# Weight splitting at seven jobs per five slots, a later input chain for the second pair, and the low-part branch at slot 24

## The chip, the cores and the metric

One core of one Trainium2 chip runs the whole program. The metric is device microseconds of one execution, and the time of a kernel is the median of its runs. A profiled execution has its own time and a span, from the first to the last of the program's instructions.

## The reference, cut to what matters

A transformer block on x of 16 sequences x 256 tokens x 256 features: attention with 16 heads of 128, then a mixture of 64 experts, each behind a layernorm and each followed by one. The change touches the attention alone:

```python
w = codes * jnp.repeat(scales, block_size, axis=0)      # wq, wk, wv: 256 x 2048; wo: 2048 x 256
q = x @ w_q + bq;  k = x @ w_k + bk;  v = x @ w_v + bv   # x is layernorm(input)
scores = jnp.einsum('bqhd,bkhd->bhqk', q, k) / jnp.sqrt(128)
attn = jax.nn.softmax(scores, axis=-1)
out = jnp.einsum('bhqk,bkhd->bqhd', attn, v)
return out @ w_o + bo
```

## The kernel before, in words

**Tiling.** The 16 sequences go as 8 pairs (bp), each with 16 heads, so there are 128 items i = bp * 16 + head, and two units u (one per sequence of the pair) for each item: 256 units. The attention is a software pipeline of slots, one unit per slot. Every engine walks the same slots in order and does, in each, what the tables ORDER (lines 45 to 57) list for even and odd slots, each with its lag. An even slot of TensorE holds nearly everything for two units: scores of u and u+1 (L1029), the Q and K projection of a later head (L1000), the output projection (L1061), a V projection (L1015), and the product of probabilities and V (L1044). I call an even slot with the odd one behind it a pair of slots. VectorE takes row maxima (L1397), reciprocals (L1393), copies K out (L1372) and makes the low halves of V (L1377) and O (L1403). ScalarE does the exponentials (L1259), the high half of P (L1268), Q (L1230), V (L1237) and O (L1251). GpSimd normalises P (L931, "norm") and makes its low half (L936, "P"): in an odd slot norm(u-1), norm(u), P(u-1), P(u). SyncE issues the transposing DMA of P (L798, "T"), one unit per slot, with a lag of one slot, behind the slot's "bg" work.

**Passes.** Operands are split into a high and a low fp16 part, and a product takes three passes (high*high, high*low, low*high). The weights come as codes times scales and mostly fit the high part alone. A flag says whether any low part is nonzero; if none is, PE leaves out the pass over the weight's low part (`passes`, L981). Slots 0 to 31 always take three passes. In front of slot 32 PE waits for the flag (L1082), reads it and branches.

**Weight jobs.** 32 jobs (`w_job`, L478) make the split weights. Each is two loads of 128 x 512 f32 (codes and scales, 256 KB each, L489 or L492) into a ring of NST = 8 stages, a multiply on GpSimd (L506), a high part on ScalarE (L510), a low part on VectorE (L514), and on VectorE an OR of the low part's bits into `lowbits` (L521). Jobs below 6 run ahead of the slots; 6 to 13 stand at slots 0, 1, 1, 2, 3, 3, 4, 4, and job n from 14 on at slot n - 10, so the last is at slot 21. The loads are issued in the same slot as the multiply, in SyncE's "bg" part, which in an odd or even slot stands before T of the unit before. ScalarE's part is one slot later and VectorE's two slots later for n of 14 and above. The load of job n waits until job n - 8 has made its low part.

**Flag.** `flag_jobs` (L531) reduces `lowbits` on VectorE at slot 25, transposes it on PE at slot 27 (L537), and reduces again at slot 28 (L538, L540).

**Input chain.** `x_jobs(bp)` (L450) computes the layernorm of pair bp and transposes it into XT: small VectorE steps (L357 to L388), four ScalarE steps (L392), and twice a PE transpose (L423) with its high and low copies (L427, L429). It is spread by the table PLACE["x"] over slots base + 1 to base + 14 with base = (bp - 1) * 32. For bp = 1 its products are first used by V in slot 26 and by Q and K in slot 30. A K projection waits for the last use of its bank bP1 in front of it, so it waits for a transpose's low copy.

**Zero fills.** SyncE also fills BUF in DRAM with zeros in slots 24, 26, 28 and 30 (L808, 1926 KB each), behind the slot's T, and Y from slot 32 on (L823, 512 KB each). They go through the same SyncE DMA queue as T.

Of the kernel before, what the change touches and what calls it, by code (L numbers as in the profile page):

```python
# [18 lines left out]
E = 64  # L19
CAP = 96  # L20
NST = 8
SCALE = 128.0 ** -0.5

SX, SW, SV, SP_, SO = 4.0, 4.0, 2.0, 64.0, 128.0
# [69 lines left out]


TURN_X = (11, 13)
PE_AT = (17, 19, 23, 31)
STORE_AT = (18, 20)
KEEP_AT = (22, 24)
# [26 lines left out]
def places(chain, base):  # L126

    left = {who: iter(slots) for who, slots in PLACE[chain].items()}

    def at(who):  # L130
        slot, j = next(left[who])
        return base + slot, j

    return at
# [49 lines left out]
def build(nc, x, wc, wsc, wo_c, wo_s, bqkv, bo, gateT, sguT, sdT, ewT, ewd, out):  # L184
    ctx = ExitStack()
    with ctx:
# [249 lines left out]
        def k_read(slot):  # L436

            return (s["kl"], sum(i < FIRST["K"] or k_place(i) < pe_place(slot, "bg") for i in range(NI)))
# [11 lines left out]
        def x_jobs(bp):  # L450
            g = bp % 4
            base = (bp - 1) * 32

            def load(eng):
                if bp >= 4:
                    eng.wait_ge(s_x1[bp % 2], 32 * ((bp - 4) // 2 + 1))
                eng.dma_start(X[:, g, :, :], x[bp * 512:(bp + 1) * 512, :].rearrange("(t p) d -> p t d", p=128)
                              ).then_inc(s_x[g], 16)

            plan["sp"].setdefault(PRO if bp < 3 else base, []).append(load)  # L460
            at = places("x", base) if bp else first
            put(stats, XC, 0, at, lambda t: X[:, g, t, :], [(s_x[g], 16 * (bp // 4 + 1))])
            put(normal, XC, 0, at, lambda t: XN[:, t, :], lambda t: X[:, g, t, :])
            for c in range(2):
                slot = base + TURN_X[c] if bp else PRO
                w = [k_read(slot)] if bp else [(s["cg"], 2)]
                turn(XC, slot, at, lambda t, c: XN[:, t, c * 128:(c + 1) * 128], c,
                     lambda l, c=c: XT[:, bp % 2, l, c, :], w, [(s["k"], max(0, 16 * (bp - 1)))])
            xt_ready[bp] = XC.n
# [8 lines left out]
        def w_job(n):  # L478
            m, chn, c = wjobs[n]
            b = n % NST  # L480
            slot = PRO if n < 6 else {6: 0, 7: 1, 8: 1, 9: 2, 10: 3, 11: 3, 12: 4, 13: 4}.get(n, n - 10)

            def load(eng):
                if n >= NST:
# [9 lines left out]
                                      ).then_inc(s_st[b], 16)  # L494

            cnt = 2 * (n // NST + 1)
            plan["sp"].setdefault(slot, []).append(load)
            if m < 3:
                o = c * 2048 + chn * 512
            else:  # L500
# [20 lines left out]
                    eng.scalar_tensor_tensor(out=lowbits, in0=lo.bitcast(U32), scalar=NOSIGN, in1=lowbits,  # L521
                                             op0=ALU.bitwise_and, op1=ALU.bitwise_or).then_inc(s["lf"], 1)

            now = n < 14
            plan["pool"].setdefault(PRO if n < NST else slot, []).append(scaled)
            plan["act"].setdefault(slot if now else slot + 1, []).append(high)
            plan["dve"].setdefault(slot if now else slot + 2, []).append(low)
            w_ready[wjobs[n]] = n + 1


        def flag_jobs():  # L531
            def rows(eng):
                eng.wait_ge(s["lf"], 32)
                return eng.tensor_reduce(low1, lowbits, AX, ALU.max)

            LC.step("dve", 25, rows)
            LC.step("pe", 27, lambda e: e.transpose(bP1[0:1, 0:128], low1, ident[:, :]), [k_read(27)])  # L537
            n = LC.step("dve", 28, lambda e: e.tensor_reduce(low2, bP1[0:1, 0:128], AX, ALU.max))  # L538
            p1_busy[27] = (LC.sem, n)
            return LC.step("dve", 28, lambda e: e.tensor_scalar(low3, low2, 1.0, None, ALU.min))  # L540


        ht_ready, acc_free, a_free = {}, {}, {}
# [433 lines left out]
        def _(eng):  # L977
# [100 lines left out]
                for u in slots:  # L1078
                    slot_work("pe", u, work)

            attention(range(0, 32), True)
            eng.wait_ge(s["lc"], LOW_READY)  # L1082
            low = eng.value_load(low3[0:1, 0:1], min_val=0, max_val=1)
            with eng.If(low == 0):
                attention(range(32, END), False)
            with eng.Else():
                attention(range(32, END), True)

            def shared_up(k):
                g, j = divmod(k, 3)  # L1090
# [448 lines left out]
```

## Time and profile before

| | us |
|---|---|
| median of 3 runs | 1377.25 (1375.5 to 1378.28) |
| profiled execution, its own time | 1383.52 |
| its span | 1381.8 |
| PE busy in the span | 1223.8 (89%) |
| POOL busy | 922.2 (67%) |
| DVE busy | 869.4 (63%) |
| ACT busy | 826.4 (60%) |

Start times of slots are read from the first score matmul (L1029) of each even slot on PE's timeline: slot 0 at 37.40, 2 at 44.12, 4 at 54.59, 6 at 70.22, 8 at 78.53, 10 at 87.96, 18 at 128.93, 20 at 137.23, 24 at 156.40, 26 at 164.63, 32 at 189.82, 34 at 196.40 and 36 at 202.90 us. In what follows "s24" is the start of slot 24. Views show engines as PE (matmul), PEld (weight load), DVE (VectorE), ACT (ScalarE), POOL (GpSimd), and SPq (SyncE's queue); "bank" is a PSUM bank, and HT is the memory in which the weight stages lie.

### The profile page before, as it was taken

To read this page: it belongs to the slowest core of one execution; us is meant where nothing else is said; L and a number is where in the kernel's file an instruction comes from. 1 tells how busy PE (TensorE), PEld (TensorE's weight loads), DVE (VectorE), ACT (ScalarE), POOL (GpSimd) and SP (SyncE) were. 2 spreads that over 40 slices of the span, in tenths; PEclk is the share of its full clock that TensorE was granted. 3 is DMA by queue.
4 is the path that set the end of the run, shared out by engine and by line. 5 is a ranking of instruction groups with operands and counts; after the bars stand their busy time and mean duration, and the time that the engine had idled before them with its cause. 6 is when DMAs were issued, how large, how long until landed. Compare 5 with 4: busy or idle time off the path is not lost.

```text
span 1381.8 us, 25355 instructions
## 1 busy us (share of the span) xinstructions
PE 1223.8 (89%) x7876; PEld 855.4 (62%) x7876; DVE 869.4 (63%) x2285; ACT 826.4 (60%) x2128; POOL 922.2 (67%) x1126
## 2 busy tenths in 40 slices
PE   3789999999899999989999998998966998989984
PEld 1455666666566666666666666666634577768863
DVE  5766667677668758777976875777765333223337
ACT  2566668778677767777777677777733332223413
POOL 3576656568877877887887798688755523444554
PEclk9999999999999999999999999999977999999977
DMA  5556796755655444444535444444434569887683
GB/s 189 138 150 171 188 243 165 162 95 120 120 104 107 89 98 96 77 89 93 97 69 91 94 82 79 78 79 80 88 84 132 160 176 239 225 229 206 135 251 122
DMA packets 364678, 182.68 MB, mean 132 GB/s; under 512 B 287440, under 2 KB 343222, under 8 KB 364544
## 3 DMA queue, kind: packets, MB, share of 16 engines
q1 hardware_dynamic: 344960, 166.18, 50.8%
q0 software_dynamic: 16416, 11.70, 4.6%
q10 hardware_dynamic: 3168, 3.15, 0.7%
q8 instruction: 67, 1.10, 0.3%
q14 instruction: 67, 0.55, 0.1%
HBM read 75.32 MB, written 64.69 MB: 101 GB/s over the span
## 4 chain that ended last, share of the span: by engine, by line
PE 40%; DVE 20%; DMA 13%; POOL 12%; issue 7%; ACT 5%; SPq 2%; another core or an unknown queue 0%; ACTq 0%; POOLq 0%; DVEq 0%
PE bank L1029 7%; PE bank L1000 6%; PE bank L1044 6%; DMA PT<-PH 5%; DMA Y<-W,wix 5%; POOL P L931 4%; POOL PH L936 4%; PE bank L1015 4%; DVE nm L1397 3%; PE bank L1061 3%; PE bank L1163 3%; PE bank L1106 3%; PE bank L1176 2%; PE bank L1122 2%; POOL BUF L691 2%
## 5 line engine op out<-in xcount | busy, mean ns | idle before, releaser
L931 POOL TENSOR_SCALAR P<-P,rr 128x256 f32<-128x256 f32 x512 | 245.1, 491 | 148.1 <-DVE rr L1393 139.7
L1259 ACT ACTIVATE P<-bank,nm 128x256 f32<-128x256 f32 x512 | 237.6, 469 | 153.6 <-DVE nm L1397 143.3
L936 POOL TENSOR_TENSOR PH<-P,PH 128x512 f16<-128x512 f32 x256 | 297.7, 1178 | 16.3 <-ACT PH L1268 15.5
L1000 PE MATMUL bank<-RB,W 128*128 128x512 f16 x1092 | 261.0, 382 | 12.4 <-ACT Sx L620 4.1
L691 POOL DMA_INDIRECT BUF<-RT,ix x192 | 198.3, 1033 | 96.3 <-issue 40.9
L1029 PE MATMUL bank<-RB 128*128 128x256 f32 x1024 | 246.4, 384 | 2.9 <-ACT RB L1230 1.7
L1044 PE MATMUL bank<-PT,RB 128*128 128x256 f16 x1536 | 197.7, 274 | 29.8 <-DMA PT<-PH 26.5
L1397 DVE TENSOR_REDUCE nm<-bank 128x2 f32<-128x512 f32 x256 | 174.3, 681 | 53.8 <-PE bank L1029 53.3
L1029 PEld LDWEIGHTS bank<-RB 128*128 128x128 f32 x1024 | 186.4, 192 | 26.5 <-issue 2.7
L1044 PEld LDWEIGHTS bank<-PT,RB 128*128 128x128 f16 x1536 | 146.4, 98 | 88.0 <-DMA PT<-PH 41.5
L1268 ACT ACTIVATE PH<-P 128x512 f16<-128x512 f32 x256 | 161.3, 630 | 59.1 <-POOL P L931 45.7
L1000 PEld LDWEIGHTS bank<-RB,W 128*128 128x128 f16 x1092 | 106.4, 98 | 134.3 <-issue 18.0
L952 POOL DMA_INDIRECT Y<-W,wix x64 | 90.5, 1415 | 124.3 <-ACT W L1330 76.2
L1061 PE MATMUL bank<-W,O 128*128 128x256 f16 x1080 | 142.6, 276 | 30.3 <-DVE O L1403 26.8
L1061 PEld LDWEIGHTS bank<-W,O 128*128 128x128 f16 x1080 | 104.0, 99 | 79.2 <-DVE O L1403 25.9
L1377 DVE SCALAR_TENSOR_TENSOR RB<-bank,RB 128x512 f16<-128x512 f32 x128 | 87.9, 687 | 93.1 <-ACT RB L1237 85.7
L1015 PE MATMUL bank<-W,RB 128*128 128x512 f16 x550 | 140.5, 381 | 3.3 <-DVE RB L1377 3.3
L1259 ACT ACTIVATION_READ_ACCUMULATOR P<-bank,nm 128x1 f32 x512 | 101.1, 197 | 0.0
L1403 DVE SCALAR_TENSOR_TENSOR O<-bank,bqk,O 128x512 f16<-128x512 f32 x128 | 94.8, 740 | 3.6 <-issue 3.2
L1372 DVE TENSOR_SCALAR RB<-bank,bqk 128x512 f32<-128x512 f32 x128 | 95.4, 745 | 1.9 <-PE bank L1000 1.9
L1251 ACT ACTIVATE O<-bank,bqk 128x512 f16<-128x512 f32 x128 | 87.4, 683 | 14.6 <-PE bank L1044 8.4
L1230 ACT ACTIVATE RB<-bank,bqk 128x512 f32<-128x512 f32 x128 | 87.9, 687 | 3.0 <-PE bank L1000 3.0
(200 smaller groups left out, 1609.6 us busy)
## 6 DMA issues: line engine op xcount, KB each, us to landing
RB<-in_ewT SPq DMA_DIRECT2D x24, 352.0 KB
BUF<-zrow SPq DMA_DIRECT2D x4, 1926.0 KB, 8.6
W<-BUF SPq DMA_DIRECT2D x64, 120.4 KB
HT<-in_ewT SPq DMA_DIRECT2D x18, 352.0 KB
HT<-in_wc SPq DMA_DIRECT2D x24, 256.0 KB, 4.2
HT<-in_ws SPq DMA_DIRECT2D x24, 256.0 KB, 4.6
Y<-zrow SPq DMA_DIRECT2D x10, 512.0 KB, 3.2
RB<-in_ewd SPq DMA_DIRECT2D x24, 176.0 KB
```

The source lines that it names most:

```text
L691: eng.indirect_dma_start(BUF, bass.IndirectOffsetOnAxis(ap=ix[:, rt, t, k:k + 1], axis=0), RT[:, rt, t, :], None, bounds_check=CAP * E - 1 ...
L931: r = eng.tensor_scalar(p, p, rr[:, w % 4, t:t + 1], SP_, ALU.mult, ALU.mult)
L936: eng.tensor_tensor(PH[:, w % 2, 1, :], P[:, w % 2, :], PH[:, w % 2, 0, :], ALU.subtract).then_inc(s["pl"], 1)
L1000: r = eng.matmul(bk_[:, :], W[:, m, a, c * 2048 + h * 128:c * 2048 + (h + 1) * 128], XT[:, bp % 2, b, c, :], start=(k == 0), stop=(k == n ...
L1015: r = eng.matmul(bV[:, :], XT[:, bp % 2, a, c, t * 128:(t + 1) * 128], W[:, 2, b, c * 2048 + hg * 512:c * 2048 + (hg + 1) * 512], start=(k ...
L1029: r = eng.matmul(bS[u % 2][:, t * 256:(t + 1) * 256], QK[:, i % 2, 0, q * 256 + t * 128:q * 256 + (t + 1) * 128], QK[:, i % 2, 1, q * 256: ...
L1044: r = eng.matmul(bO[:, q * 256:(q + 1) * 256], V[:, i // 4 % 2, a, 2 * q + kc, h % 4 * 128:(h % 4 + 1) * 128], PT[:, u % 2, b, :, kc, :], ...
L1061: r = eng.matmul(bACC[q][:, t * 256:(t + 1) * 256], O[:, a, q * 256 + t * 128:q * 256 + (t + 1) * 128], W[:, 3, b, h * 256:(h + 1) * 256], ...
L1259: r = eng.activation(P[:, u % 2, t * 256:(t + 1) * 256], bS[u % 2][:, t * 256:(t + 1) * 256], ACT.Exp, bias=nm0[:, u % 4, t:t + 1], accum_ ...
L1268: eng.activation(PH[:, w % 2, 0, :], P[:, w % 2, :], ACT.Copy).then_inc(s["ph"], 1)
L1372: eng.tensor_scalar(QK[:, i % 2, 1, :], bP1[:, :], 1.0 / (SX * SW), bqk[:, 1, h:h + 1], ALU.mult, ALU.add).then_inc(s["kl"], 1)
L1397: eng.tensor_reduce(nm0[:, u % 4, :], bS[u % 2][:, :].rearrange("p (t k) -> p t k", t=2), AX, ALU.max, negate=True).then_inc(s["mx"], 1)
```

## The change

- The job table. Jobs below 6 stay ahead of the slots, 6 and 7 go to slots 0 and 1, and jobs 8 to 31 go to the slots of W_AT: seven jobs in each five slots from slot 0 on, the last at slot 16. In pairs of slots these are 3, 3, 3, 3, 2, 3, 3, 3, 1.
- W_LEAD: for n >= 8 the load is issued one slot ahead of the multiply, ScalarE's part one slot behind it and VectorE's two.
- The input chain of bp = 1 moves by 12 slots: it starts at slot 13, has its transposes on PE at 23 and 25, and ends on VectorE in slot 26.
- The flag's steps move from 25, 27, 28 to 19, 21, 22, and the branch from 32 to 24.

```diff
@@ -19,6 +19,10 @@
+W_AT = (0, 0, 1, 2, 2, 3, 4, 5, 5, 6, 7, 7, 8, 9, 10, 10, 11, 12, 12, 13, 14, 15, 15, 16)
+W_LEAD = (1, 1, 2)
+FLAG_AT = 19
+BRANCH_AT = 24
@@ -94,6 +98,7 @@
 TURN_X = (11, 13)
+X_SHIFT = 12
@@ x_jobs
-            at = places("x", base) if bp else first
+            begin = base + (X_SHIFT if bp == 1 else 0)
+            at = places("x", begin) if bp else first
...
-                slot = base + TURN_X[c] if bp else PRO
+                slot = begin + TURN_X[c] if bp else PRO
@@ w_job
-            slot = PRO if n < 6 else {6: 0, 7: 1, 8: 1, 9: 2, 10: 3, 11: 3, 12: 4, 13: 4}.get(n, n - 10)
+            slot = PRO if n < 6 else n - 6 if n < NST else W_AT[n - NST]
...
-            plan["sp"].setdefault(slot, []).append(load)
+            plan["sp"].setdefault(slot if n < NST else max(0, slot - W_LEAD[0]), []).append(load)
...
-            now = n < 14
+            act_at, dve_at = (slot, slot) if n < NST else (slot + W_LEAD[1], slot + W_LEAD[2])
             plan["pool"].setdefault(PRO if n < NST else slot, []).append(scaled)
-            plan["act"].setdefault(slot if now else slot + 1, []).append(high)
-            plan["dve"].setdefault(slot if now else slot + 2, []).append(low)
+            plan["act"].setdefault(act_at, []).append(high)
+            plan["dve"].setdefault(dve_at, []).append(low)
@@ flag_jobs
-            LC.step("dve", 25, rows)
-            LC.step("pe", 27, lambda e: e.transpose(bP1[0:1, 0:128], low1, ident[:, :]), [k_read(27)])
+            LC.step("dve", FLAG_AT, rows)
+            LC.step("pe", FLAG_AT + 2, lambda e: e.transpose(bP1[0:1, 0:128], low1, ident[:, :]), [k_read(FLAG_AT + 2)])
...
@@ tensor block
-            attention(range(0, 32), True)
+            attention(range(0, BRANCH_AT), True)
             eng.wait_ge(s["lc"], LOW_READY)
             low = eng.value_load(low3[0:1, 0:1], min_val=0, max_val=1)
             with eng.If(low == 0):
-                attention(range(32, END), False)
+                attention(range(BRANCH_AT, END), False)
             with eng.Else():
-                attention(range(32, END), True)
+                attention(range(BRANCH_AT, END), True)
```

## Rows read from the trace of the kernel before

**Rows 1.** The page: span, and busy time of each engine
```profile
span 1381.8 us, 25355 instructions
PE 1223.8 (89%) x7876; PEld 855.4 (62%) x7876; DVE 869.4 (63%) x2285; ACT 826.4 (60%) x2128; POOL 922.2 (67%) x1126
```
**Rows 2.** Busy time by stretch, one line per pair of slots, from slot 0
```profile
core 0: us, PE busy (x) PEld busy (x) DVE busy (x) ACT busy (x) POOL busy (x), PEclk, DMA share, GB/s
37.40:44.12 6.72, 5.78 (x27) 3.10 (x26) 4.98 (x12) 4.64 (x14) 2.34 (x5) 1.00 0.00 1
44.12:54.59 10.47, 7.49 (x38) 4.21 (x39) 9.34 (x21) 5.57 (x15) 7.32 (x8) 0.99 0.76 200
54.59:70.22 15.63, 11.80 (x51) 7.38 (x51) 10.85 (x24) 7.50 (x19) 11.20 (x13) 0.79 0.64 170
...
78.53:87.96 9.43, 8.50 (x52) 5.39 (x51) 6.45 (x11) 6.74 (x17) 6.73 (x8) 1.00 0.65 162
```
**Rows 3.** The chain of waits through slots 8 and 10: start, us, what
```profile
80.71 1.23 SPq L798
...
81.98 0.58 SPq L489
...
82.60 3.69 DMA HT<-in_ws
...
86.36 1.27 POOL HT L506
87.63 1.82 POOL P L931 x4
89.45 1.13 POOL PH L936
...
90.60 1.23 SPq L798
```
**Rows 4.** GpSimd's timeline in slots 8 to 10: start, us, [idle before it <- what ended it]
```profile
82.20 1.45 POOL L506 TENSOR_TENSOR HT<-HT 128x512 f32<-128x512 f32 x1
86.36 1.27 POOL L506 TENSOR_TENSOR HT<-HT 128x512 f32<-128x512 f32 x1 [2.70 <-DMA HT<-in_ws]
87.61 1.85 POOL L931 TENSOR_SCALAR P<-P,rr 128x256 f32<-128x256 f32 x4
89.42 2.72 POOL L936 TENSOR_TENSOR PH<-P,PH 128x512 f16<-128x512 f32 x2
```
**Rows 5.** The chain where PE alone sets the pace with three passes
```profile
158.29 2.59 PE bank L1000 x12
160.88 1.31 PE bank L1061 x12
162.19 1.30 PE bank L1015 x6
163.49 1.31 PE bank L1044 x12
164.80 1.73 PE bank L1029 x8
```
**Rows 6.** Who waited on PE from 70 to 146 us: total, times, longest
```profile
PE bank L1000 <- DVE RB L429: 2.9, 2, 1.5
```
**Rows 7.** VectorE's timeline in slots 8 and 9: the two jobs' steps
```profile
80.44 0.79 DVE L514 SCALAR_TENSOR_TENSOR W<-HT,W 128x512 f16<-128x512 f32 x1
81.26 1.27 DVE L521 SCALAR_TENSOR_TENSOR C<-W,C 128x256 uint32<-128x256 uint32 x1
...
85.08 0.42 DVE L521 SCALAR_TENSOR_TENSOR C<-W,C 128x256 uint32<-128x256 uint32 x1
```
**Rows 8.** Busy time by stretch: pairs of slots 24, 26, 28, 30, and 36
```profile
156.40:164.63 8.23, 8.23 (x52) 5.55 (x51) 5.30 (x10) 4.95 (x14) 4.82 (x7) 1.00 0.83 231
164.63:172.98 8.35, 8.35 (x54) 5.64 (x53) 4.07 (x9) 4.96 (x14) 4.18 (x7) 1.00 1.08 309
172.98:181.59 8.61, 8.39 (x53) 5.48 (x51) 3.83 (x10) 5.05 (x13) 4.17 (x6) 1.00 1.14 273
181.59:189.82 8.23, 8.23 (x52) 5.53 (x51) 3.62 (x8) 4.94 (x14) 4.15 (x6) 1.00 1.07 307
...
202.90:209.44 6.54, 6.54 (x43) 4.48 (x41) 6.09 (x18) 4.95 (x14) 3.90 (x7) 1.00 0.66 161
```
**Rows 9.** Zero fill of BUF: its time to landing; weight load waiting for T in slot 32
```profile
DMA to landing us min/median/max: 7.9/8.6/9.2
195.73 0.55 PEld L1044 LDWEIGHTS bank<-PT,RB 128*128 128x128 f16 x6 [0.18 <-DMA PT<-PH]
```

More of the change, by code:

```diff
@@ L534, in rows @@
                 return eng.tensor_reduce(low1, lowbits, AX, ALU.max)
-            LC.step("dve", 25, rows)
-            LC.step("pe", 27, lambda e: e.transpose(bP1[0:1, 0:128], low1, ident[:, :]), [k_read(27)])
-            n = LC.step("dve", 28, lambda e: e.tensor_reduce(low2, bP1[0:1, 0:128], AX, ALU.max))
-            p1_busy[27] = (LC.sem, n)
-            return LC.step("dve", 28, lambda e: e.tensor_scalar(low3, low2, 1.0, None, ALU.min))
+            LC.step("dve", FLAG_AT, rows)
+            LC.step("pe", FLAG_AT + 2, lambda e: e.transpose(bP1[0:1, 0:128], low1, ident[:, :]), [k_read(FLAG_AT + 2)])
+            n = LC.step("dve", FLAG_AT + 3, lambda e: e.tensor_reduce(low2, bP1[0:1, 0:128], AX, ALU.max))
+            p1_busy[FLAG_AT + 2] = (LC.sem, n)
+            return LC.step("dve", FLAG_AT + 3, lambda e: e.tensor_scalar(low3, low2, 1.0, None, ALU.min))
         ht_ready, acc_free, a_free = {}, {}, {}
```

## The prediction, made before the changed kernel was run

> **What bounds the kernel now.** I read the page's span and busy shares first [rows 1]: PE is busy for 89% of the span and no other engine for more than 67%, so over the whole program PE is near its bound, and a change that doesn't take PE work away can only win where PE waits. The change touches slots 0 to 32 only, some 150 us, so I cut that part into pairs of slots [rows 2, 8]. The reader is to see three stages there. In the pairs of slots 24 to 30 the length is 8.23 to 8.61 us and PE is busy all of it or nearly [rows 8]. The chain of waits says the same from the other side: with three passes the five groups of matmuls of a pair follow one another without a gap, 2.59 + 1.31 + 1.30 + 1.31 + 1.73 = 8.24 us [rows 5]. With two passes a pair is 6.54 [rows 8]. From slot 8 to slot 24, though, a pair takes longer: (156.40 - 78.53) / 8 = 9.73 us, for example 9.43 with 8.50 of it busy on PE [rows 2]. And slots 2 to 6 are the worst: 10.47 and 15.63 us, with the granted clock at 0.79 in the second, as PE had idled [rows 2].
>
> What ends last in the 9.73 us pairs is read from the chain, and it is a loop that leaves PE out [rows 3]: T's issue on SyncE (1.23), the issue of an even slot's weight load (0.58 and a second issue), the transfer (3.69 to landing), the multiply on GpSimd (1.27), four normalisations (1.82), one P low part (1.13), and T again, 9.89 us for one turn. GpSimd's own timeline shows the hole: idle for 2.70 us in front of L506, ended by the load's landing [rows 4]. The reason is in the code: the load of even slot s stands behind T(s-2) in SyncE's queue, T(s-2) waits for GpSimd's low part of unit s-2, and GpSimd's next work after that is the multiply that needs this load. So the load's whole latency lies on the path once per pair.
>
> **The change part by part.** Load one slot earlier: for an even slot s it now stands in SyncE's slot s-1, behind T(s-3) and in front of T(s-2). T(s-3) needs a low part that GpSimd made a pair earlier, so the load has a full pair (over 8 us) against 3.69 us of transfer [rows 3]. The loop is cut and the 2.70 us hole goes. The ring's wait does not come back in its place: the load of job n waits for the low part of job n-8, which stands at least two slots ahead of it in the new table. Queued behind a load in SyncE is T; three loads a pair are three times some 1.2 us of issue beside 2 x 1.23 for the Ts, about 6 us in a pair of over 8, so the queue isn't full. Cover for the load is gone only if SyncE falls back by a pair; then the 2.70 returns.
>
> What is late next in a pair with three jobs? Three candidates. PE: 8.24 [rows 5]. GpSimd: its pair with two jobs is 1.45 + 1.27 + 1.85 + 2.72 = 7.29 us of work [rows 4], a third job adds 1.27 to 1.45, so 8.6 to 8.7. VectorE: 6.45 busy with two jobs [rows 2], a third adds 0.79 + 0.42 up to 0.79 + 1.27 [rows 7], 7.7 to 8.5, and it has to wait for others in between. I take 8.7, GpSimd's, for a pair with three jobs, and PE's 8.24 for others.
>
> L521 takes 0.42 us in one place and 1.27 in another with the same shape [rows 7], and the long one lies beside L506 and L936 of GpSimd: at 82.20 the multiply also took 1.45 instead of 1.27, and the two L936 took 2.72, although one is 1.13 in the chain [rows 3, 4]. The Trainium skill, "SBUF — State Buffer", section "SBUF: two separate sides", says why and speaks against this change: a VectorE instruction with two SBUF inputs and a GpSimd instruction that reads SBUF share a port pair, an exclusive lock that is held for a whole instruction. The trace agrees with blocks of that size. By that rule a denser stream of jobs would make more such blocks, which is rival B below; its price is worked out there from rows.
>
> Stage by stage, from the starts of slots:
>
> - Slots 0 to 4, 37.40 to 54.59, 17.19 us now. After: slot 0's pair stays 6.7 (nothing of GpSimd's or SyncE's ended late there [rows 2]), slot 2's pair is a three-job pair, 8.7, because jobs 8 to 12 are loaded before unit 0's T is even due. 15.4; gain 1.8. Job 7's load is now queued behind the loads of 8, 9 and 10, which wait for the first stages; it moves by over 10 us, and GpSimd had been idle there until 41 us, so I cost it at nothing. If it were later than 41 it would cost its lateness.
> - Slots 4 to 8, 54.59 to 78.53, 23.94 us now. GpSimd's loads for slot 4's jobs came late there. After: 2 x 8.7 = 17.4; gain 6.5. The low clock of that stretch [rows 2] goes with the idle time.
> - Slots 8 to 18, 78.53 to 128.93, 50.40 us now. After: one pair at 8.24 and four at 8.7, 43.0. To this come the small VectorE steps of the input chain, which move from slots 1 to 6, where they lay in the bad stretch, to slots 13 to 18: 19 steps, most of 0.15 us, of which a few are blocked by GpSimd for up to about a microsecond. I take 1.4 for them, between 0 (all in VectorE's idle time) and 3. 44.4; gain 6.0.
> - Slots 18 to 24, 128.93 to 156.40, 27.47 us now. No jobs after slot 18; PE's 3 x 8.24, plus 0.5 for the transpose in slot 23 and for the flag's transpose: 25.2; gain 2.3. The transposes' waits on K (2.9 us for the two now [rows 6]) were inside pairs that GpSimd's loop held up, so taking them from slots 11 and 13 gives nothing by itself; at 23 and 25 they lie at PE's own pace and cost 0.4 to 1.5 each. The second one falls into the next stage.
>
> Sum up to slot 24: 1.8 + 6.5 + 6.0 + 2.3 = 16.6 us.
>
> - Branch at 24: four pairs of slots with two passes. If PE stayed the bound they would fall from 8.23 + 8.35 + 8.61 + 8.23 = 33.42 to 4 x 6.54 = 26.16, a gain of 7.3, less up to 1 for the transposes. But exactly in these pairs SyncE fills BUF with zeros, and the DMA engines are busy all the time: a share of 1.07 to 1.14 and 273 to 309 GB/s from slot 26 on, against 0.66 and 161 in slot 36 [rows 8]. A pair moves 309 x 8.35 = 2.58 MB; these bytes don't depend on PE, and at the highest rate seen they take 8.2 to 8.4 us. The zero fill lands 7.9 to 9.2 us after its issue, and in slot 32 the weight load for L1044 waited for T [rows 9]: the Ts come out behind the fill. Each T(u) is needed by PE in slot u+2, and ScalarE's P high part waits for the T two units earlier, so PE can't run ahead by more than a pair. So the four pairs stay at about 8.3 each, and what PE saves turns into waits for T. s24 to s34 is 40.0 now; after it is 4 x 8.3 + 6.5 = 39.7. Gain 0.3. Bounds: +7.3 if the Ts come through anyway, and -1.5 if a T behind a fill finds no slack where it had 2 us of it.
>
> The Trainium skill, "DMA: Bandwidth & Descriptors", section "Queues, rings and completion order", says that descriptors of one ring are consumed in order, and SyncE's transfers all go into one row of rings; by that the T behind a fill waits for the fill, and the wait for T in slot 32 agrees. A gain of 7.3 would need T to pass the fill.
>
> The branch itself: it now stands behind the flag of slot 22 by two slots where it had four, a pair's time, and the flag's steps on VectorE are done in the first half of slot 22. In slot 32 PE showed no gap at it. I cost it at nothing; late, it would cost at most a pair's rest, some 4 us. V of slot 26 needs the input chain's last step in the same slot's start on VectorE, some 3 us ahead of V's turn; cost nothing, and in the DMA-bound stage a wait of 2 us would be hidden.
>
> Total 16.6 + 0.3 = 16.9. Against the profiled execution's own 1383.52 that is 1366.6, and against the median of 1377.25, which lies 6.3 below it, 1360.4. I predict 1360.5.
>
> **The rivals.**
>
> A, forecast (0.63): as above, 1360.5; with its unknown terms 1357 to 1364.
>
> B (0.18): the port between VectorE and GpSimd gives back most. Then the three-job pairs, eight of them from slot 2 to 18, stay at 9.7, as in the two-job pairs now. s24 = 37.40 + 6.7 + 8 x 9.7 + 25.2 = 146.9, a gain of 9.5, so 1367.7. For it: the block of 0.85 us in one L521 [rows 7]. Against it: two-job pairs have 2.70 us of idle GpSimd time inside [rows 4], which is not work. The skill's page above is what speaks for it.
>
> C (0.13): the DMAs don't bind in slots 24 to 32, and the branch pays 5 to 7 us on top: 1360.5 - 6 = 1354.5. The DMA share over 1 speaks against it [rows 8].
>
> D, slower (0.03): VectorE, ScalarE and GpSimd lock into a serial chain in dense pairs, as in slot 4's pair now, which had four jobs and took 15.63 us [rows 2], 3.9 a job. Three jobs would make 11.7 a pair, and seven such pairs cost 7 x 3.0 = 21 more than I take: 1381, slower by 4. It decides from 8.7 + 16.9 / 7 = 11.1 us a pair. Against it: that pair's GpSimd idled for its loads, which are early now.
>
> E (0.03): the change doesn't do what it says, as a wait in SyncE's queue (the ring or T) holds the loads as late as now; the pairs stay at 9.73 and only the shorter stretch of jobs helps. Gain about 1 to 5.
>
> **How the numbers follow.** The likeliest is A, 1360.5. The range has to leave out no more than 2 in 10: from C's 1354.5 to a little over B's 1367.7, 1354.5 to 1368.5. A measurement of this kernel tells 0.2%, 2.75 us, from no change. A, B, C and most of E are faster by more: 0.96. Same 0.01, slower 0.03.
>
> **What would show it.** In the changed profile: slot 24 starts near 156.4 - 16.6 = 140; no idle time of GpSimd in front of L506 between slots 4 and 16; three-job pairs of 8.5 to 9; in the pairs of slots 24 to 30 a length near 8.3, a DMA share over 1 and waits of L1044 for T, although L1000 counts 8 matmuls a pair. If these pairs are 6.6, C is right. If POOL is fully busy in pairs of 9.7, B is. It would be wrong altogether if SyncE's queue held T back behind a load that waits for a free stage.

## The result, and the profile after

| | before | after |
|---|---|---|
| median, us | 1382.14 (9 runs, 1375.50 to 1386.71) | 1371.16 (9 runs, 1366.08 to 1375.49) |
| profiled execution: own time; span | 1383.52; 1381.8 | 1371.37; 1369.6 |

The ratio of after to before is 0.9927, 95% interval 0.9900 to 0.9955: the change is faster by 10 us, between 6 and 14. I had forecast 16.9 us less and a time of 1354.5 to 1368.5. The direction was right, the size was not.

The page of the changed kernel (span; busy time and share of each engine), to be held against [rows 1]:

```profile
span 1369.6 us, 25270 instructions
PE 1215.2 (89%) x7836; PEld 850.2 (62%) x7836; DVE 873.8 (64%) x2285; ACT 825.7 (60%) x2128; POOL 925.9 (68%) x1126
```

PE has 40 instructions less, the passes of four pairs of slots that the earlier branch leaves out, and is busy 8.6 us less. Where it is busy less is read from two stretches, slots 0 to 24 and 24 to 34, before (first two lines) and after (last two), with the columns of [rows 2]:

```profile
37.40:156.40 119.00, 101.60 (x574) 64.62 (x572) 84.50 (x157) 73.22 (x187) 85.05 (x95) 0.97 0.60 151
156.40:196.40 40.00, 39.78 (x244) 26.71 (x242) 21.52 (x45) 24.72 (x66) 21.14 (x31) 1.00 1.05 276
38.05:150.28 112.23, 98.16 (x571) 62.78 (x570) 94.40 (x160) 73.05 (x185) 92.18 (x99) 1.00 0.60 141
150.28:190.02 39.74, 33.98 (x206) 22.81 (x205) 19.88 (x41) 25.44 (x67) 19.94 (x30) 1.00 1.07 278
```

The branch takes 5.8 us from PE in slots 24 to 34 (39.78 to 33.98). Another 3.4 us go in slots 0 to 24 with the same work: nearly all in slot 4's pair, where PE was busy 11.80 us at a granted clock of 0.79 before and 8.64 us at 1.00 after. The question is what became of the 5.8 us.

Busy time by stretch, one line per pair of slots (slots 2, 4, 6, then 12, 14, 16, 18), answers to [rows 2]:

```profile
core 0: us, PE busy (x) PEld busy (x) DVE busy (x) ACT busy (x) POOL busy (x), PEclk, DMA share, GB/s
45.38:55.33 9.95, 7.34 (x39) 4.30 (x39) 8.45 (x12) 6.54 (x17) 9.51 (x10) 1.00 0.68 159
55.33:67.07 11.74, 8.64 (x51) 5.47 (x51) 10.71 (x16) 7.07 (x18) 9.67 (x10) 1.00 0.83 176
67.07:75.30 8.23, 8.23 (x52) 5.55 (x51) 6.94 (x11) 6.34 (x16) 8.15 (x9) 1.00 0.99 262
...
92.88:103.14 10.26, 8.69 (x52) 5.31 (x51) 9.19 (x15) 6.86 (x18) 10.26 (x11) 1.00 0.79 208
103.14:114.11 10.97, 8.63 (x50) 5.47 (x51) 10.79 (x25) 7.25 (x18) 9.14 (x10) 1.00 0.75 186
114.11:122.81 8.70, 8.40 (x53) 5.49 (x51) 8.56 (x17) 6.00 (x17) 8.19 (x10) 1.00 0.35 71
122.81:132.88 10.07, 8.46 (x50) 5.55 (x51) 9.02 (x17) 6.66 (x17) 6.01 (x7) 1.00 0.28 54
```

The reader is to see three kinds of pair: GpSimd busy for all of it (10.26 of 10.26), VectorE busy for nearly all of it (10.79 of 10.97), and pairs that no engine fills, with VectorE the nearest (10.71 of 11.74 in slot 4, 9.02 of 10.07 in slot 18). With the same starts of slots as before, the stages came out so:

| slots | before | forecast | after |
|---|---|---|---|
| 0 to 4 | 17.19 | 15.4 | 17.28 |
| 4 to 8 | 23.94 | 17.4 | 19.97 |
| 8 to 18 | 50.40 | 44.4 | 47.51 |
| 18 to 24 | 27.47 | 25.2 | 27.47 |
| 0 to 24 | 119.00 | 102.4 | 112.23 |
| 24 to 34 | 40.00 | 39.7 | 39.74 |

So the profile shows 7.0 us for the part that the change touches, in place of 16.9. The two spans differ by 12.2: another 5.8 us lie behind slot 34, where the kernels are the same, and 0.6 are lost again as the slots began later.

**The holes that went, and what filled the time.** GpSimd's timeline in slots 7 to 11 of after, against [rows 4] (start, us):

```profile
72.41 2.60 POOL L937 TENSOR_SCALAR P<-P,rr 128x256 f32<-128x256 f32 x4
74.98 2.72 POOL L942 TENSOR_TENSOR PH<-P,PH 128x512 f16<-128x512 f32 x2
77.66 4.35 POOL L512 TENSOR_TENSOR HT<-HT 128x512 f32<-128x512 f32 x3
81.99 2.60 POOL L937 TENSOR_SCALAR P<-P,rr 128x256 f32<-128x256 f32 x4
84.56 2.71 POOL L942 TENSOR_TENSOR PH<-P,PH 128x512 f16<-128x512 f32 x2
87.24 4.34 POOL L512 TENSOR_TENSOR HT<-HT 128x512 f32<-128x512 f32 x3
91.57 2.01 POOL L937 TENSOR_SCALAR P<-P,rr 128x256 f32<-128x256 f32 x4
```

No idle time is left in front of L512 (L506 before), so the loop through the load is cut, as forecast. But a turn with three jobs takes 81.99 - 72.41 = 9.58 us and 91.57 - 81.99 = 9.58 again, not 8.7: the three multiplies take 1.45 each and the four normalisations 2.60 where they took 1.85 [rows 4]. The next turn, from 91.57 to 100.55, takes 8.98. Over the eight pairs of slots 2 to 18 the mean is (122.81 - 45.38) / 8 = 9.68 us a pair.

**Slots 24 to 34.** The same view there (slots 24, 26, 28, 30, 32), against [rows 8]:

```profile
150.28:157.21 6.93, 6.93 (x46) 5.01 (x45) 4.14 (x8) 5.32 (x14) 3.94 (x7) 1.00 0.95 262
157.21:163.72 6.51, 6.51 (x43) 4.59 (x42) 3.91 (x8) 5.29 (x14) 3.67 (x6) 1.00 1.08 299
163.72:172.36 8.64, 6.85 (x43) 4.40 (x41) 3.43 (x8) 4.83 (x14) 4.02 (x7) 1.00 1.13 258
172.36:180.72 8.36, 6.85 (x43) 4.41 (x41) 3.89 (x8) 5.19 (x14) 4.50 (x7) 1.00 1.06 306
180.72:190.02 9.30, 6.85 (x42) 4.41 (x41) 4.51 (x11) 4.80 (x13) 3.80 (x6) 1.00 1.12 268
```

and PE's and SyncE's timelines, with the wait in brackets, against [rows 9]:

```profile
170.83 1.69 PE L1050 MATMUL bank<-PT,RB 128*128 128x256 f16 x12 [1.76 <-DMA PT<-PH]
178.65 0.83 PE L1050 MATMUL bank<-PT,RB 128*128 128x256 f16 x6 [0.94 <-DMA PT<-PH]
188.48 1.70 PE L1050 MATMUL bank<-PT,RB 128*128 128x256 f16 x12 [2.41 <-DMA PT<-PH]
```

```profile
172.76 4.82 SPq L804 DMA_TRANSPOSE PT<-PH  x2
177.67 0.91 SPq L814 DMA_DIRECT2D BUF<-zrow  x1
```

The first two pairs run at PE's own 6.93 and 6.51, although the DMA share is already 0.95 and 1.08. In the next three it stays over 1 and PE waits for T once or twice a pair, with only 6.85 of 8.4 to 9.3 us busy. These waits are 5.7 us in all, as much as PE's work fell, so PE's saving turned into waits. The bytes tell the same: 278 GB/s over 39.74 us after and 276 over 40.00 before are both 11.0 MB.

### The profile page after: what moved, and what is told of

The parts are those of the page before. It is cut to its first block, busy times and chain, and to the rows that moved or that the text cites. A ratio compares the mean times of both kernels' runs of the same rounds, so it can differ in the third digit from the quotient of the medians.

```text
span 1369.6 us, 25270 instructions
## 1 busy us (share of the span) xinstructions
PE 1215.2 (89%) x7836; PEld 850.2 (62%) x7836; DVE 873.8 (64%) x2285; ACT 825.7 (60%) x2128; POOL 925.9 (68%) x1126
## 4 chain that ended last, share of the span: by engine, by line
PE 38%; DVE 20%; DMA 14%; POOL 12%; issue 8%; ACT 5%; SPq 1%; another core or an unknown queue 1%; ACTq 0%; POOLq 0%; DVEq 0%
DMA PT<-PH 7%; PE bank L1035 7%; DMA Y<-W,wix 6%; PE bank L1050 6%; PE bank L1006 6%; POOL P L937 4%; POOL PH L942 4%; DVE nm L1403 4%; PE bank L1021 4%; PE bank L1067 3%; PE bank L1169 3%; PE bank L1128 2%; PE bank L1112 2%; PE bank L1182 2%; POOL BUF L697 2%
## 5 line engine op out<-in xcount | busy, mean ns | idle before, releaser
L937 POOL TENSOR_SCALAR P<-P,rr 128x256 f32<-128x256 f32 x512 | 249.2, 498 | 140.1 <-DVE rr L1399 131.7
L942 POOL TENSOR_TENSOR PH<-P,PH 128x512 f16<-128x512 f32 x256 | 295.8, 1170 | 20.5 <-ACT PH L1274 19.4
L1006 PE MATMUL bank<-RB,W 128*128 128x512 f16 x1076 | 257.2, 381 | 9.0 <-ACT Sx L626 4.3
L1006 PEld LDWEIGHTS bank<-RB,W 128*128 128x128 f16 x1076 | 104.9, 98 | 128.5 <-issue 16.9
L1067 PE MATMUL bank<-W,O 128*128 128x256 f16 x1064 | 138.8, 274 | 23.1 <-DVE O L1409 19.9
L1257 ACT ACTIVATE O<-bank,bqk 128x512 f16<-128x512 f32 x128 | 87.3, 682 | 15.4 <-PE bank L1050 8.4
```

The lines of the kernel that those rows point to most:

```text
L937: r = eng.tensor_scalar(p, p, rr[:, w % 4, t:t + 1], SP_, ALU.mult, ALU.mult)
L942: eng.tensor_tensor(PH[:, w % 2, 1, :], P[:, w % 2, :], PH[:, w % 2, 0, :], ALU.subtract).then_inc(s["pl"], 1)
L1006: r = eng.matmul(bk_[:, :], W[:, m, a, c * 2048 + h * 128:c * 2048 + (h + 1) * 128], XT[:, bp % 2, b, c, :], start=(k == 0), stop=(k == n ...
L1067: r = eng.matmul(bACC[q][:, t * 256:(t + 1) * 256], O[:, a, q * 256 + t * 128:q * 256 + (t + 1) * 128], W[:, 3, b, h * 256:(h + 1) * 256], ...
```

## The experiments

Each time is set against runs of the kernel before on the same chip. The changed kernel gave a ratio of 0.9927 on one chip and 0.9894 on another, so differences under 0.4% between two of these ratios, taken on different chips, can't be told apart. The pairs of slots in the profiles tell more, as most of them repeat within some tenths of a microsecond. Their sum is less sure: four profiles of programs that are the same up to slot 24 (the changed kernel twice, the branch at 32, the fill in pieces) took 111.7 to 113.9 us from slot 0 to 24.

Part of that spread is TensorE's clock. In the changed kernel's second profile slot 6's pair takes 9.66 us with PE busy for all of it, at a granted clock of 0.85 (0.50, the lower of its two levels, 1.2 GHz, from 67.20 to 69.00 us); in the first it takes 8.23 us at 1.00. PE had waited for a T just before in both, 3.08 and 3.00 us, so the same wait was followed by the lower level in one profile and not in the other. Where it comes it costs a pair 1.4 to 1.7 us, so a pair is to be read with its PEclk.

**The kernel before, profiled again.**

> The kernel before, unchanged, profiled once more. It shows how far a profiled execution differs from another of the same kernel, and where. Theory 1 (the profiled execution of before was a long one, and the extra lies behind slot 34, where both kernels are the same): slots 0 to 34 take 159.0 us again within 1, and from slot 34 to the end it is 1170 to 1180 us in place of 1185. Theory 2 (the change shortens slots behind 34 by some later effect): 1183 us or more again.

Its span is 1372.5, 9.3 less than that of the first profile; its ratio to the kernel before is 1.0008 (0.9979 to 1.0036), as it should be for the same program. Busy time by stretch: slots 0 to 24, 24 to 34, and the rest; the last line is the same stretch of the first profile of before.

```profile
36.54:155.89 119.35, 100.37 (x573) 63.38 (x572) 84.61 (x157) 73.24 (x187) 85.21 (x95) 0.99 0.62 151
155.89:195.82 39.93, 39.71 (x243) 26.81 (x242) 21.60 (x45) 24.80 (x66) 20.64 (x30) 1.00 1.07 277
195.82:1372.50 1176.68, 1070.57 (x7027) 759.63 (x7025) 744.35 (x2046) 718.17 (x1861) 801.54 (x977) 0.97 0.55 125
```

```profile
196.40:1381.80 1185.40, 1070.55 (x7027) 759.11 (x7025) 744.77 (x2046) 718.89 (x1861) 803.43 (x977) 0.97 0.55 124
```

Theory 1 holds: slots 0 to 34 are 159.3 us (159.0 in the first), and behind slot 34 it is 1176.7 in place of 1185.4, with the same busy time on PE to 0.02 us. Slot 4's pair takes 15.53 us with PE at 0.89 and busy for 10.30, against 15.63 with 11.80 at 0.79 in the first, so the low clock wasn't what made it long. The profiled execution of before was a long one in a part that the change doesn't touch. Over all fourteen profiles of this case that part takes 1170.1 to 1185.4 us. So one profile against another shows the stages well and the total badly.

**The early loads alone.** The kernel before, with this edit:

```diff
-            plan["sp"].setdefault(slot, []).append(load)
+            plan["sp"].setdefault(slot if n < NST else max(0, slot - 1), []).append(load)
```

> The kernel before with one edit: the loads of jobs 8 and above stand one slot earlier in SyncE's queue; job table, input chain, flag and branch stay. Theory 1 (the load's latency in GpSimd's loop was the cost, and with two jobs a pair GpSimd's work fits under PE's 8.24 us): the pairs of slots 8 to 22 fall from 9.73 to 8.3 to 8.5 us, slot 4's pair from 15.6 to under 12; slot 24 starts 13 to 17 us earlier than before and the whole is 13 to 17 us faster, which is more than the full change gave (10 us). Theory 2 (the port between VectorE and GpSimd takes the gain back in any dense stretch): the pairs stay at 9.2 or more and the gain is under 6 us.

Ratio 0.9953 (0.9929 to 0.9976), 6.5 us: half of what theory 1 wanted. In slots 8 to 24 it was near, (148.78 - 79.34) / 8 = 8.68 us a pair in place of 9.73, where I had said 8.3 to 8.5. Two of these pairs, slots 12 and 16:

```profile
96.59:105.74 9.15, 8.82 (x56) 5.88 (x55) 8.15 (x13) 6.35 (x16) 7.65 (x9) 1.00 0.78 175
114.49:123.03 8.54, 8.39 (x52) 5.48 (x51) 7.59 (x12) 5.87 (x16) 7.64 (x9) 1.00 0.76 187
```

The miss is slot 4's pair, which grew from 15.63 to 17.07 us with no wait for a load's landing left in it. In the changed kernel it is 11.74, so there its new job table and lags helped, not its earlier loads (the moved input chain isn't needed for it: 11.39 with the chain back, below). Slots 0 to 24 take 112.8 us, against 112.2 in the full change: for the stretch up to slot 24, the one-line edit is worth as much as the whole.

**Loads early, and the parts of jobs 8 to 13 spread.** On top of the last, ScalarE's and VectorE's parts of jobs 8 to 13 one slot later:

```diff
-            plan["act"].setdefault(slot if now else slot + 1, []).append(high)
-            plan["dve"].setdefault(slot if now else slot + 2, []).append(low)
+            plan["act"].setdefault(slot if n < NST else slot + 1, []).append(high)
+            plan["dve"].setdefault(slot + 2 if not now else slot if n < NST else slot + 1, []).append(low)
```

> The kernel before with the loads one slot earlier, and ScalarE's and VectorE's parts of jobs 8 to 13 one slot behind GpSimd's multiply in place of in the same slot. With the loads alone, slot 4's pair stayed at 17.06 us (15.63 before), and nothing there waited for a load's landing. Theory 1 (what made that pair long is that ScalarE waits in the same slot for GpSimd's multiply, with the exponential of unit 5 queued behind, and VectorE for ScalarE): slot 4's pair falls to 10 to 13 us, and slot 0 to 24 from 112.8 to 106 to 109 us. Theory 2 (four jobs in one pair are too much work wherever they stand): it keeps 15 us or more.

Inconclusive. Slot 4's pair fell to 11.80 us, but slot 6's rose from 8.80 to 14.51, so slots 0 to 24 are 112.7 us as before this edit; ratio 0.9945 (0.9929 to 0.9962). The edit made a wait of its own: K of slot 6 is the first use of job 13, and PE stood idle for 3.32 us until 73.68, just behind that job's low part, which VectorE ended at 73.57. What made slot 4's pair long in the kernel before isn't settled by this run.

**The branch back at 32** in the changed kernel (`BRANCH_AT = 32`):

> The changed kernel with its branch back at slot 32, all else as changed. Theory 1 (in slots 24 to 32 the zero fill of BUF and the transposes queued behind it set the pace, and the earlier branch only turns PE's work into waits for T): same time as the changed kernel within 1 us; the stretch from slot 24 to slot 34 is 39.7 to 40.3 us, against 39.74 in the changed kernel. Theory 2 (the branch pays): slower than the changed kernel by 3 to 7 us.

Slots 24 to 34 take 39.94 us with three passes, against 39.74 with two. Slot 26:

```profile
156.95:165.18 8.23, 8.23 (x52) 5.55 (x51) 3.93 (x8) 5.42 (x14) 3.78 (x6) 1.00 1.14 283
```

PE is busy throughout, with the DMA share over 1.1 as well. The branch is worth 0.2 us here, which can't be told from nothing: the changed kernel's second profile has 40.64 for this stretch. Ratio 0.9953 (0.9931 to 0.9974), which overlaps with the changed kernel's first, 0.9900 to 0.9955, and not with its second, 0.9861 to 0.9928, both from other chips.

**The zero fill in 16 pieces** in the changed kernel:

```diff
-                if 24 <= slot < 32 and slot % 2 == 0:
+                if 24 <= slot < 56 and slot % 2 == 0:
...
-                    eng.dma_start(BUF[n * 1536:(n + 1) * 1536, :].rearrange("(k p) c -> p k c", p=128),
-                                  zrow[:, :].unsqueeze(1).broadcast_to([128, 12, ROW])).then_inc(s["bi"], 16)
+                    eng.dma_start(BUF[n * 384:(n + 1) * 384, :].rearrange("(k p) c -> p k c", p=128),
+                                  zrow[:, :].unsqueeze(1).broadcast_to([128, 3, ROW])).then_inc(s["bi"], 16)
```

> The changed kernel with the zero fill of BUF in 16 pieces of 482 KB, one in each even slot from 24 to 54, in place of four of 1926 KB in slots 24 to 30. Theory 1 (DMA-bound pairs): the pairs of slots 28 to 32 fall from 8.64, 8.36 and 9.30 us to 6.5 to 6.7, slot 24 to slot 34 takes 33 to 34 us in place of 39.7, and the whole is 5 to 7 us faster than the changed kernel. Theory 2 (PE waits for T for another reason, such as the late P high part): these pairs keep 8 us or more and the time stays within 1.5 us of the changed kernel.

Slots 26, 28 and 30:

```profile
155.47:161.97 6.50, 6.50 (x43) 4.56 (x41) 3.91 (x8) 5.29 (x14) 3.67 (x6) 1.00 0.64 158
161.97:169.39 7.42, 6.68 (x43) 4.50 (x41) 3.77 (x8) 5.08 (x14) 4.38 (x7) 1.00 0.62 139
169.39:175.89 6.50, 6.50 (x42) 4.57 (x41) 3.33 (x7) 4.93 (x13) 4.15 (x6) 1.00 0.64 157
```

The DMA share falls to 0.64 and the pairs to 6.50, with one wait of 0.7 us for T left. Slots 24 to 34 take 33.86 us, 5.9 less than in the changed kernel, and 34.07 and 34.09 in two later runs that have the same pieces. Ratio 0.9890 (0.9864 to 0.9916), median 1359.76; on the same chip the branch at 32 with the large fills had 1369.20. This shows that the large fill held these pairs, and that with it gone the branch does pay. Whether the bytes count or the long entry in front of T isn't parted, as the edit takes both away; the wait of 0.7 us comes at a share of 0.62.

**The same fill with the early loads alone**, branch at 32:

> The kernel before with the loads one slot earlier and the zero fill in 16 pieces; branch at 32. It parts what the branch can give from what the fill costs. Theory 1: against the loads alone (e2) it gains 0 to 1.5 us only, since with three passes PE needs 8.23 us a pair in slots 24 to 30 anyway, and only the pair of slot 32 had a wait for T. Theory 2 (the fill costs PE more than its waits show): 3 us or more faster than e2.

39.93 us from slot 24 to 34, against 40.70 with the large fills: 0.8 less, as theory 1 had it. Ratio 0.9939 (0.9917 to 0.9961). With the changed kernel and the two runs on it above this makes a square for slots 24 to 34: large fill, branch 32: 39.94; large fill, branch 24: 39.74; small pieces, branch 32: 39.93 (here on the old job table and chain); small pieces, branch 24: 33.86. Either edit alone gives nothing, both together 6.

**The input chain back** at slots 1 to 14 in the changed kernel (`X_SHIFT = 0`):

> The changed kernel with the input chain of the second pair back at slots 1 to 14. Theory 1 (the chain's small VectorE steps, moved among the last jobs, made VectorE the bound in slots 14 to 20): the pairs of slots 14 to 18, 10.97, 8.69 and 10.07 us in the changed kernel, fall to 8.3 to 9.5, and the pairs of slots 2 to 10 grow by as much; slot 0 to 24 stays 112.2 us within 1.5, as the same steps meet the same locks. Theory 2 (moving the chain behind the jobs did help): slot 0 to 24 grows by 3 us or more.

Slots 0 to 24 take 112.19 us against 112.23: the same, as in theory 1. Slots 16 and 18 fall to PE's 8.23 each from 8.70 and 10.07, and slots 4 and 6 take 11.39 and 9.92 in place of 11.74 and 8.23. But 1.7 us of slot 6's is the clock, with PE busy for all of it at 0.83, and slot 2's pair ran at 0.83 too; so the equal sums don't show that the move is worth nothing, only that it is worth no more than some 2 us either way. Slot 14's pair stayed long, 11.54, where I had expected 9.5 at most: PE waits 2.68 us for a T in it, which the next run is about. Ratio 0.9943 (0.9917 to 0.9970).

**Loads grouped.** In the changed kernel with the fill in pieces:

```diff
-            plan["sp"].setdefault(slot if n < NST else max(0, slot - W_LEAD[0]), []).append(load)
+            plan["sp"].setdefault(slot if n < NST else max(0, slot - (slot + 1) % 2), []).append(load)
```

> The changed kernel with the zero fill in 16 pieces and the loads of odd slots moved from one slot ahead into their own slot, so that all loads of a pair stand in front of both of the pair's Ts while SyncE waits for P, and none between the two. Theory 1 (in slot 4 PE waited 3.0 us for a T that was issued and transferred behind two jobs' loads): slot 4's pair falls from 11.76 to 9 to 10 us and slot 0 to 24 from 111.7 to 108 to 110 us; 2 to 3 us faster than with the fill in pieces alone. Theory 2 (DMA traffic as such delays the Ts): no change within 1 us.

What it is about is seen in the changed kernel's SyncE and PE timelines in slots 4 and 5:

```profile
56.76 1.23 SPq L804 DMA_TRANSPOSE PT<-PH  x1
58.03 0.73 SPq L495 DMA_DIRECT2D HT<-in_wc  x1
58.80 0.45 SPq L495 DMA_DIRECT2D HT<-in_ws  x1
59.29 0.43 SPq L498 DMA_DIRECT2D HT<-in_oc  x1
59.77 0.47 SPq L498 DMA_DIRECT2D HT<-in_os  x1
60.34 1.23 SPq L804 DMA_TRANSPOSE PT<-PH  x1
```

```profile
66.40 0.83 PE L1050 MATMUL bank<-PT,RB 128*128 128x256 f16 x6 [3.00 <-DMA PT<-PH]
```

Four loads stand between the two Ts, and PE goes on 6 us after the second T's issue. With all loads in front of both Ts PE waits for no T from slot 4 to slot 18: slot 4's pair is 9.93 us against 11.76 in the kernel with the fill in pieces, slot 14's 9.95 against 11.01. What is left of slot 4's pair over 8.24 is the clock:

```profile
53.74:63.67 9.93, 9.93 (x50) 6.74 (x51) 8.90 (x14) 7.05 (x18) 9.49 (x10) 0.83 0.70 168
```

PE is busy for all of it, at 0.50 in its first 1.8 us. Before it PE had idled 2.78 us until VectorE had copied K out (53.63), behind the low parts and ORs of two jobs. From slot 0 to 24 it is 110.24 against 111.70, 1.5 us less where I had said 2 to 3; part came back in slots 10 and 16, 9.58 against 8.78 and 9.67 against 8.67. In the total it can't be told: ratio 0.9897 (0.9854 to 0.9941).

**One SBUF input.** In the changed kernel the OR (in0 and lowbits) becomes a `tensor_scalar` AND of one input:

> The changed kernel with the OR into lowbits replaced by an AND of the low part alone, so that this VectorE instruction reads one SBUF tensor in place of two, of the same shape; the flag then stands for the last job's low part only. Theory 1 (two SBUF inputs lock GpSimd out and are locked out by it): this instruction takes 0.40 to 0.45 us in each of its 24 places, GpSimd's turn with three jobs falls from 9.6 to 9.2 us or less, and slot 0 to 24 falls by 3 to 8 us. Theory 2 (the long ones are long for another reason): durations up to 1.3 us stay and so does slot 0 to 24.

Theory 1 fails in the form in which I wrote it. The instruction took 0.29 to 1.25 us (the OR 0.42 to 1.38), so one input in place of two doesn't spare it the long waits. It is shorter when free, 0.29, GpSimd's turns are 9.19, 9.18 and 8.74 in place of 9.58, 9.58 and 8.98, and slots 0 to 24 take 109.70 us, 2.5 less; theory 2, which wanted that sum unchanged, fails too. The Trainium skill, "SBUF — State Buffer", section "Who interferes with whom", lists `tensor_scalar` among those that can enter a 2-port mode and contend with GpSimd when their operands allow it; durations both shorter than and as long as the OR's agree with that, and it makes this a bad probe of the port. Ratio 0.9880 (0.9827 to 0.9933), from four runs.

**Most of the ORs left out** of the changed kernel:

```diff
-                if n == 0:
+                if n % 8 == 0:
...
-                else:
-                    eng.wait_ge(s["lf"], n)
-                    eng.scalar_tensor_tensor(out=lowbits, in0=lo.bitcast(U32), scalar=NOSIGN, in1=lowbits,
-                                             op0=ALU.bitwise_and, op1=ALU.bitwise_or).then_inc(s["lf"], 1)
```

> The changed kernel with the OR into lowbits left out for 28 of the 32 jobs (kept, as a plain AND, for jobs 0, 8, 16 and 24), so the flag no longer covers all low parts. It takes away 21 of the 24 VectorE instructions of that line behind slot 0 and the blocks they make. Theory 1 (VectorE and GpSimd hold each other up over their shared port, in proportion to such instructions): GpSimd's turn with three jobs falls from 9.6 us towards 8.9, the longest pairs of slots 12 to 18 (10.27, 10.97, 10.07) lose 1 us each or more, slot 0 to 24 falls from 112.2 to 105 to 108.5 us. Theory 2 (GpSimd's long turn is its own work): slot 0 to 24 keeps 110 us or more.

Slots 0 to 24 take 109.27 us, between the two theories' numbers. GpSimd's timeline:

```profile
70.59 2.27 POOL L934 TENSOR_SCALAR P<-P,rr 128x256 f32<-128x256 f32 x4
72.83 2.71 POOL L939 TENSOR_TENSOR PH<-P,PH 128x512 f16<-128x512 f32 x2
75.51 4.22 POOL L512 TENSOR_TENSOR HT<-HT 128x512 f32<-128x512 f32 x3
79.72 2.27 POOL L934 TENSOR_SCALAR P<-P,rr 128x256 f32<-128x256 f32 x4
```

The first turn is 9.13 us in place of 9.58, and three turns from slot 7 on take 27.3 us in place of 28.1: the ORs account for 0.3 us of a turn in the mean. The low part (L520), with two SBUF inputs too, is still there. Of the pairs that repeat within 0.1 us in the four profiles with the ORs, three fell: slot 2's from 9.95 to 8.90, slot 12's from 10.26 to 8.88, slot 18's from 10.07 to 8.23. But slot 14's rose from 10.97 to 11.62, with PE 2.66 us idle for a T, and slot 16's from 8.70 to 9.92, with PE busy for all of it at a clock of 0.83. So the sum hides a part of what the ORs cost. The edit also spares VectorE the ORs' own time, and the run doesn't part this from the holding up. How the two engines hold each other is best read from one place of the changed kernel, slot 14's pair:

```profile
103.22 2.27 POOL L942 TENSOR_TENSOR PH<-P,PH 128x512 f16<-128x512 f32 x2
104.54 1.50 DVE L520 SCALAR_TENSOR_TENSOR W<-HT,W 128x512 f16<-128x512 f32 x1
105.45 1.71 POOL L512 TENSOR_TENSOR HT<-HT 128x512 f32<-128x512 f32 x1
106.07 1.37 DVE L527 SCALAR_TENSOR_TENSOR C<-W,C 128x256 uint32<-128x256 uint32 x1
```

GpSimd's L942 ends at 105.49; VectorE's L520, 0.67 us when free, ends at 106.04, that is 0.55 after it. GpSimd's L512, 1.27 when free, starts at 105.45 and takes 1.71; VectorE's L527, 0.42 when free, ends at 107.44, some 0.3 after L512's end at 107.16. The ends fit, within 0.2 us, each instruction doing its work only behind the other engine's whole one, in turn. Between 69 and 110 us of the changed kernel, eleven ORs had a mean of 1.12 us. Ratio of the run without them: 0.9902 (0.9867 to 0.9937), median 1370.56 beside the changed kernel's 1371.11 on the same chip: in the total the 3 us can't be seen.

**The chain tightened.** On top of the grouped loads, the chain's steps ahead of its transposes two slots later (for bp = 1, `slot + 2 if slot < begin + 9 else slot`):

> The changed kernel with the fill in 16 pieces, the loads grouped, and the first part of the second pair's input chain (statistics and the four normalising steps) two slots later, at 15 to 22 in place of 13 to 20; its transposes stay at 23 and 25. Theory 1 (in slots 14 to 20 VectorE is the bound because the chain meets the last jobs): the four pairs of slots 12 to 18, 39.95 us together in the grouped kernel, lose 1 to 3 us and slot 0 to 24 falls from 110.2 to 107.5 to 109. Theory 2 (the sum over the dense stretch is what counts, wherever the chain lies): no change within 0.7 us.

Theory 1's numbers were met: the pairs of slots 12 to 18 take 38.04 us against 39.95, and slots 0 to 24 108.32 against 110.24. The clearest is slot 18's pair, 9.43, which was 10.07 in all five profiles with the chain two slots earlier. What VectorE's load does there is read in the changed kernel, slot 18's pair:

```profile
127.93 0.47 ACT L1265 ACTIVATE P<-bank,nm 128x256 f32<-128x256 f32 x1 [3.41 <-DVE nm L1403]
128.97 1.47 PE L1067 MATMUL bank<-W,O 128*128 128x256 f16 x12 [1.61 <-DVE O L1409]
129.59 2.46 POOL L937 TENSOR_SCALAR P<-P,rr 128x256 f32<-128x256 f32 x4 [3.98 <-DVE rr L1399]
```

All three other engines wait for VectorE. This kernel is the shortest of the case in slots 0 to 34, 142.4 us, and has the lowest ratio, 0.9847 (0.9808 to 0.9885), an interval that overlaps with those of the kernels with the fill in pieces and of the changed kernel. Its median is 1366.32 where before was 1385.15 and the changed kernel 1371.11 on the same chip.

**The changed kernel again.**

> The changed kernel once more, for the size of its gain beside the others on one chip and for a second profile. If the gain is what slots 0 to 34 show, 159.1 - 152.0 = 7.1 us, the ratio to before is near 0.995; if the first comparison's 0.9927 is the true one, the gain is 10 us. In the profile slot 0 to 24 is 112.2 and slot 24 to 34 is 39.7 us again.

Ratio 0.9894 (0.9861 to 0.9928), 14.7 us. Slots 0 to 24 took 113.93 us and 24 to 34 40.64 in this profile, more than in the first (slot 6's pair was 9.66 in place of 8.23, by the clock). So its profile shows a gain of 4.4 us up to slot 34, its time one of 10 to 19. The 7.1 us (a ratio near 0.995) is ruled out, the 10 us lies just inside the interval, and the two stages came out longer than the 112.2 and 39.7 that I gave.

## Why the prediction was right or wrong

The step that failed is a term of the sum: the length of a pair in the stretch with the jobs. I took 8.7 us for a pair with three jobs and 8.24 for the others, and the pairs of slots 2 to 18 took 9.68. By stages the sum missed 1.9 us in slots 0 to 4, 2.6 in 4 to 8, 3.1 in 8 to 18 and 2.3 in 18 to 24, 9.8 in all up to slot 24, and nothing in slots 24 to 34.

**That the load's latency made the 9.73 us pairs: right.** GpSimd's holes went, and the early loads alone took these pairs to 8.68.

**A pair with three jobs at 8.7: wrong, the largest miss.** I added one undisturbed multiply to a turn of 7.29 and called GpSimd's 8.7 the bound. Measured turns are 9.58, 9.58 and 8.98. The multiplies (1.45 each) and normalisations (2.60 for four) stretch, and VectorE's ORs have a mean of 1.12. The size is that of rival B, 9.7, to which I gave 0.18 and which the 9.68 of slots 2 to 18 meets (a part of that is waits for T, next paragraph); the sign that I had named for B, GpSimd busy for all of a long pair, is there too (10.26 of 10.26); its condition was on record in the row with 1.27 us for an OR of 0.42 [rows 7], and I argued against it with GpSimd's idle time, which says nothing on what is left once that is filled. Leaving out most ORs returned 0.3 us a turn and 3.0 us up to slot 24, so the ORs are shown as a part; that the low parts (L520) are the rest of the stretch from 8.7 is not shown. Slots 0 to 4 missed mostly for the same reason: slot 2's pair is 9.95 with the ORs and 8.90 without. The sum for slots 8 to 18 also counted four pairs with three jobs where the table has three; put right it would have been 0.5 us farther off.

**Queue time of T behind the loads: not priced.** I counted SyncE's issues, found the queue not full, and stopped there. Where an even slot of SyncE had two jobs' loads between two Ts, PE waited for T, 3.00 us in slot 4. Slots 4 to 8 came out at 19.97 against 17.4; grouping the loads gave 1.8 in slot 4's pair and 1.1 in slot 14's, and 1.5 up to slot 24.

**Slots 18 to 24 at PE's pace: wrong.** "No jobs after slot 18" overlooked that VectorE's parts stand two slots behind GpSimd's: slot 18's pair has the last one and the end of the chain's small steps, 10.07 us in place of 8.24. I had put 1.4 us on the chain in all. With the chain at its old place, slots 16 and 18 are at 8.23, and the sum up to slot 24 stays at 112.2 us, of which some 1.7 us are the clock in that profile. So the move cost at most some 2 us by itself, but the dense pairs had no room for it. Slot 22's pair was 9.06: transposes and flag cost 0.8, not 0.5.

**Slots 24 to 34, gain 0.3: right**, 39.74 against 39.7, and for the reason given. The square of four runs shows it: 40 us in three corners and 33.86 in the one with small pieces and the early branch. Hitting it to 0.1 us was luck, as the second profile has 40.64, and the pairs came out otherwise than the 8.3 each that I gave: two at PE's 6.93 and 6.51, and the waits for T in slots 28 to 32, up to 9.30.

**The base.** All sums stood on one profile. For slots 0 to 34 that was sound. But the profile of before was 9 us long behind slot 34, and the median moved too: 1377.25 from three runs, 1382.14 from nine. Of the 10.7 us between my 1360.5 and the measured 1371.16, 4.9 are this move of the median before and 5.8 the smaller gain (11.0 between the medians, where I had 16.8). With the 7.0 us of the stages, the first median would have given 1370.2, close to what was measured, but by luck: the larger gain in the total and the higher median before cancel. The forecast range ended at 1368.5 since it took the three-job pair at 9.7 as its worst case, and the other two misses come on top of that.

What stays open is the total. The stages show 7.0 us and 4.4 us in two profiles of the changed kernel, and the ratios 10 (6 to 14) and 14.7 (10 to 19). The stretch behind slot 34 varied by 15 us among profiles of programs that are the same there, so no profile can say whether it is shorter after the change by some microseconds. What makes it vary was not looked into. Nor do the runs show what, besides the ORs, keeps a pair with three jobs above 8.7.

## What to carry to other kernels

When a wait is cut out of a loop, price the loop's other members as they are under the new load, not as they are with the wait in it: the time in which an engine idled was also the time in which its neighbour ran undisturbed. In these slots a shorter PE schedule gained nothing while a large fill kept the DMA share over 1, so look at the DMA share of a stretch first, and see whether its bulk transfers can go elsewhere. In a queue count what stands between two urgent entries, beside how full the queue is.

## What the runs showed of the hardware

- A VectorE instruction with one SBUF input (`tensor_scalar` on 128 x 256 uint32) was held up as long as one with two: 0.29 to 1.25 us. I had expected 0.40 to 0.45.
- Instructions of VectorE and GpSimd stretched in both directions where they met, with ends that fit each waiting for the other's: 0.42 us became up to 1.38, 0.67 up to 1.57 on VectorE, and 1.27 became up to 1.72 on GpSimd.
- After PE had idled 3.08 us its granted clock was 0.50 for some 3 us in one profile of the changed kernel, and stayed at 1.00 after 3.00 us in another; the same pair took 9.66 and 8.23 us.
- Two profiled executions of one program differed by 9 us behind slot 34, with PE's busy time equal to 0.02 us in 1070.6.
